# The last steps of a two-layer attention kernel: the last pair's projections first, four output products behind them, one pair's residuals in the place of the normalised x

## The chip, the core and the metric

The kernel runs on one core of a Trainium2 chip. A core has five engines that run side by side, each taking its instructions in the order in which they stand: PE multiplies matrices and writes to PSUM (eight banks), DVE does elementwise work and reductions, ACT applies functions such as exp and tanh, POOL does elementwise work on SBUF, and SP here issues the transfers. They wait for each other on semaphores. The metric is the time of one execution in microseconds (us); less is better.

## The reference

Two layers are applied to `x` of 32 sequences x 128 tokens x 512 features, both with a conditioning vector per sequence. The first is softmax attention with 16 heads, the second linear attention with 8 heads. The change touches the second alone:

```python
xn = _ln(x, ln_w, ln_b)
q = softmax((xn @ Wq + bq) per head, over the head's features)
k = softmax((xn @ Wk + bk + (1 - mask) * -1e6) per head, over the tokens)
v = (xn @ Wv + bv) * mask
att = einsum('bnhd,bnhl->bhdl', k, v)
y = einsum('bnhd,bhdl->bnhl', q, att)
scale, shift = split(silu(emb) @ W_emb + b_emb)
hh = _ln(y, ln2_w, ln2_b) * (1 + scale) + shift
return x + silu(hh) @ W_out + b_out
```

(The lines are those of the reference, with reshapes written out in words.) Everything is float32. Each large product is made of three faster ones, of high and low parts of both factors.

## The kernel before

The sequences are worked on in pairs (`GROUP = 2`), 16 pairs for each layer. The work of a pair is spread over three steps: in step `i` the pair `n = i + 2` is loaded, normalised and transposed, the pair `f = i + 1` is projected to keys, values and queries, and the pair `k = i` goes through attention, the second norm and the nonlinearity; the output products of the pair before come one step later still. The order on each engine is written out by hand, in one function per engine and step (`step0`, `step_mixed`, `step1`), and the steps of a layer run in a loop. Behind the last loop stands `drain(k, f)`: no pair is left to load, `k` is the last pair but one and `f` the last, and the output products of the pair `k - 2` are still due. The change is in these five `drain` functions (SP, POOL, ACT, DVE, PE).

The parts of it, as the rest of the text names them, with lines of the kernel before:

- PE: `keys`, `values`, `queries1` (24 products of 256 columns, or 12 of 512 for one sequence, L1294 to L1296), `turn_k` and `turn_q` (transposes, L1400 and L1408), `keys_values` (L1420: k times v, eight products), `query` (L1430: q times that), `turn_yn` (L1381), `output` (12 products of 512 columns, L1294 to L1296, with `s_hi` and `s_lo`).
- DVE: `k_soft` (L1001, L1006), `q_add` and `q_soft` (L1019 to L1028), `q_sums` (L1035, L1039), `kv_out` (L1048, scales the result of `keys_values`), `y_norm` (L960, then statistics at L894 and L898), `silu` (L976), `s_low_part` (L982), `output` (L988: adds product and residual).
- ACT: `k_exps`, `q_exps`, `kt_out`, `qt_out` (copies out of PSUM), `film1` (L657), `tanh` (L665), `s_high` (L670).
- POOL: `norm2` (L468 to L495), `v_mask` (L501, L505), `residual` (L521: adds the output bias to the residual).
- SP: `load_back` (L338, the residual into `x_res`), `store` (L342).

`LATE`, `LATER` and `DRAIN` name the PSUM banks that these steps use. `xn` is the buffer of the normalised x. `x_res` has room for one pair of residuals; `x_in`, where x was loaded for the norm, still holds the last pair's x and serves as its residual. Before, a residual of the pair `k` can therefore be loaded only when the finished output of the pair `k - 2` has been stored from the same place (`load_back` waits for `stored`). Buffers of one place that decide the order: `y_s` (the input of the second norm) and `th` (tanh and silu) hold one sequence each, so that `y_norm` of a sequence waits for `norm2` of the one before, and `silu` for the `s_high` and `s_low_part` of the one before.

## Time and profile before

| | us |
|---|---|
| median of 3 runs | 1080.86 (1080.82 to 1081.48) |
| the profiled execution, its own time | 1084.61 |
| its span, first to last instruction | 1082.8 |
| PE busy | 1030.0 (95%) |
| DVE busy | 770.1 (71%) |
| ACT busy | 609.6 (56%) |
| POOL busy | 588.7 (54%) |
| mean granted TensorE clock | 0.991 |

The span is the time from the first to the last instruction of the profiled execution. An engine counts as busy while it executes; matmuls overlap, so the time that one takes in a row is longer than the distance to the next one's start, and the distance is what a sequence of them costs. The drain runs from 1026.97 us to the end.

### The profile page before, as it was taken

Reading aid. Unit: us, or ns where it says so; the run is one execution under the profiler, and the core shown is the slowest. Engines: PE = TensorE matmul, PEld = TensorE weight load, DVE = VectorE, ACT = ScalarE, POOL = GpSimd, SP = SyncE. Lnnn points to the kernel's source line nnn. Section 1 sums busy time; section 2 is a strip of 40 time slices with the busy share of each in tenths; the row PEclk is TensorE's granted clock in tenths of the full one; section 3 lists DMA queues with packets and bytes.
Section 4 is the critical chain, followed back from the end, with each engine's and each line's share of the span. In section 5 each row is a group of like instructions: output and inputs, shape, how many; then the busy total and the mean of one; then the engine's idle time right before and its main releaser. Section 6 shows DMA issues by size and latency. Waiting matters only on the chain. (4 is left out here: it accounts for less than half of the span.)

```text
span 1082.8 us, 26060 instructions
## 1 busy us (share of the span) xinstructions
PE 1030.0 (95%) x8554; PEld 897.0 (83%) x8554; DVE 770.1 (71%) x1349; ACT 609.6 (56%) x2018; POOL 588.7 (54%) x870
## 2 busy tenths in 40 slices
PE   2999999999999999999997899999999999999996
PEld 2678889888888888988886778888888888888885
DVE  3567666766667666676678687777887787778775
ACT  2375678766776668766694544444444444444443
POOL 3453465445654465544653576556655565666623
PEclk9999999999999999999999899999999999999999
DMA  7833102211012110111113312222111121112111
GB/s 210 283 138 120 62 26 63 63 41 61 24 63 63 41 55 30 63 54 50 43 45 112 103 44 65 64 65 63 54 39 62 53 63 53 53 63 63 44 40 39
DMA packets 46401, 74.24 MB, mean 69 GB/s; under 512 B 8304, under 2 KB 14576, under 8 KB 46352
## 3 DMA queue, kind: packets, MB, share of 16 engines
q1 hardware_dynamic: 46352, 73.63, 21.4%
q8 instruction: 26, 0.43, 0.2%
q14 instruction: 23, 0.19, 0.1%
HBM read 56.80 MB, written 16.81 MB: 68 GB/s over the span
## 5 line engine op out<-in xcount | busy, mean ns | idle before, releaser
L468 POOL TENSOR_SCALAR stat<-stat 128x1 f32<-128x1 f32 x128 | 34.9, 273 | 351.5 <-DVE stat L898 330.4
L1294 PE MATMUL bank<-xt_hi,w_hi 128*128 128x256 f32 x768 | 220.4, 287 | 1.5 <-DVE xt_lo L921 1.5
L1296 PE MATMUL bank<-xt_hi,w_lo 128*128 128x256 f32 x768 | 215.5, 281 | 0.0
L1295 PE MATMUL bank<-xt_lo,w_hi 128*128 128x256 f32 x768 | 215.4, 281 | 0.0
L634 ACT ACTIVATE prob<-prob,neg_max 128x128 f32<-128x128 f32 x512 | 198.5, 395 | 10.5 <-DVE neg_max L935 10.5
L1294 PE MATMUL bank<-w_hi,xt_hi 128*128 128x512 f32 x384 | 157.2, 409 | 3.6 <-DVE w_lo L859 2.0
L1296 PE MATMUL bank<-w_hi,xt_lo 128*128 128x512 f32 x384 | 151.9, 396 | 0.0
L1295 PE MATMUL bank<-w_lo,xt_hi 128*128 128x512 f32 x384 | 151.3, 394 | 0.0
L1294 PEld LDWEIGHTS bank<-xt_hi,w_hi 128*128 128x128 f32 x768 | 146.5, 191 | 5.0 <-issue 1.9
L1295 PEld LDWEIGHTS bank<-xt_lo,w_hi 128*128 128x128 f32 x768 | 146.1, 190 | 1.3
L1296 PEld LDWEIGHTS bank<-xt_hi,w_lo 128*128 128x128 f32 x768 | 145.9, 190 | 0.0
L1294 PE MATMUL bank<-w_hi,s_hi 128*128 128x512 f32 x256 | 107.1, 418 | 4.1 <-DVE s_lo L982 2.7
L665 ACT ACTIVATE th<-z_s 128x512 f32<-128x512 f32 x64 | 40.9, 638 | 115.8 <-POOL z_s L511 115.2
L657 ACT ACTIVATE z_s<-bank,film_ab 128x128 f32<-128x128 f32 x128 | 48.1, 455 | 97.2 <-PE bank L1381 94.0
L521 POOL TENSOR_TENSOR x_res<-x_res,wide 128x512 f32<-128x512 f32 x62 | 91.5, 1486 | 18.3 <-DMA x_res<-between_layers 18.3
L1296 PE MATMUL bank<-w_hi,s_lo 128*128 128x512 f32 x256 | 101.2, 396 | 0.0
L1295 PE MATMUL bank<-w_lo,s_hi 128*128 128x512 f32 x256 | 100.7, 393 | 0.0
L634 ACT ACTIVATION_READ_ACCUMULATOR prob<-prob,neg_max 128x1 f32 x512 | 99.2, 194 | 0.0
L677 ACT ACTIVATE q_t<-q_t,k_max 128x128 f32<-128x128 f32 x128 | 49.9, 391 | 86.5 <-DVE k_max L1006 86.4
L932 DVE TENSOR_TENSOR prob<-bank,mask_row 128x512 f32<-128x512 f32 x128 | 87.6, 684 | 11.5 <-PE bank L1340 10.7
L935 DVE TENSOR_REDUCE neg_max<-prob 128x4 f32<-128x512 f32 x128 | 87.8, 686 | 4.4
L642 ACT ACTIVATE room<-bank 128x512 f32<-128x512 f32 x128 | 74.2, 593 | 29.3 <-PE bank L1351 28.3
(113 smaller groups left out, 2341.8 us busy)
## 6 DMA issues: line engine op xcount, KB each, us to landing
x_in<-in_x_dram SPq DMA_DIRECT2D x32, 256.0 KB, 2.8
x_res<-in_x_dram SPq DMA_DIRECT2D x32, 256.0 KB, 2.9
between_layers<-x_res SPq DMA_DIRECT2D x32, 256.0 KB, 2.0
x_in<-between_layers SPq DMA_DIRECT2D x32, 256.0 KB, 3.2
x_res<-between_layers SPq DMA_DIRECT2D x30, 256.0 KB, 2.6
out_dram<-x_res SPq DMA_DIRECT2D x30, 256.0 KB, 2.0
room<-in_L_cond_W_emb_dram SPq DMA_DIRECT2D x8, 512.0 KB, 6.9
prob<-in_L_cond_emb_w_dram SPq DMA_DIRECT2D x4, 512.0 KB, 7.6
```

Of the source, the lines that this page charges most:

```text
L468: pool.tensor_scalar(v[:, 8:9], v[:, 7:8], EPS, None, ALU.add).then_inc(s[a_in].sem, 1)
L521: pool.tensor_tensor(buf[:, b, :], buf[:, b, :], wide[:, OUT_BIAS[l], :], ALU.add).then_inc(s["res_full"].sem, 1)
L634: last = act.activation(prob[:, b, i, :], prob[:, b, i, :], ACT.Exp, bias=neg_max[:, b, i:i + 1], accum_out=row_sum[:, b, h:h + 1])
L642: act.activation(prob_t[:, g, :], bank[FIRST["PT"][g % 2]][:], ACT.Copy).then_inc(s[f"pt_out{g}"].sem, 1)
L657: last = act.activation(z_s[:, b, c * P:(c + 1) * P], bank[bk["H"][b]][:, c * P:(c + 1) * P], ACT.Identity, bias=shift, scale=scale)
L665: act.activation(th[:], z_s[:, b, :], ACT.Tanh, scale=0.5).then_inc(s["tanh_full"].sem, 1)
L677: last = act.activation(v[:, i, :], v[:, i, :], ACT.Exp, bias=k_max[:, pair, i:i + 1], accum_out=k_sum[:, slot, pair, i:i + 1])
L932: dve.tensor_tensor(prob[:, b, heads, :], bank[c][:].rearrange("p (r n) -> p r n", r=HC0), row, ALU.add).then_inc(s[f"masked{c}"].sem, 1)
L935: dve.tensor_reduce(neg_max[:, b, heads], prob[:, b, heads, :], AX.X, ALU.max, negate=True).then_inc(s[f"neg{c}"].sem, 1)
L1294: pe.matmul(o, a_hi, b_hi, start=start, stop=False)
L1295: pe.matmul(o, a_hi, b_lo, start=False, stop=False)
L1296: return pe.matmul(o, a_lo, b_hi, start=False, stop=stop)
```

## The change

It moves instructions in the drain and gives two residuals another place:

- PE: `keys(f, 0)` stands at the head, the two output products of the pair `k - 2` move behind `turn_q(f, 0)` and `query(f, 1)`, `turn_yn(k, 0)` and `(k, 1)` behind the `keys_values` of the pair `f`, and each `turn_yn` of `f` one product forward, so that the last four products are `LATER` 0 and 1 and `DRAIN` 0 and 1. The banks are given out anew.
- DVE, ACT: the same parts in a new order that follows PE. On DVE `k_soft(f, 0)` stands ahead of `kv_out(k, 0)`, and the `y_norm` of `f` behind `silu(k, 0)` and `s_low_part(k, 0)`.
- SP: the residuals of the pair `k` are loaded into `xn`, both at once, as soon as `xn` has been transposed; they no longer wait for the stores of the pair `k - 2`.
- POOL: both residual additions of `k` stand behind `norm2(k, 1)`. A wait of POOL on its own `consts` before the start is taken out.

Three places in the order of instructions. On PE, the end of the last loop step and the start of the drain (`q_t` and `room` are keys and queries being transposed), before:

```order
L1400 MATMUL bank<-ident,q_t 128x128 x4
L1408 MATMUL bank<-ident,room 128x128 x4
L1400 MATMUL bank<-ident,q_t 128x128 x4
L1294 MATMUL bank<-w_hi,s_hi 128x512
L1295 MATMUL bank<-w_lo,s_hi 128x512
```

and with the change (line numbers of the new kernel are one higher here):

```order
L1401 MATMUL bank<-ident,q_t 128x128 x4
L1409 MATMUL bank<-ident,room 128x128 x4
L1401 MATMUL bank<-ident,q_t 128x128 x4
L1295 MATMUL bank<-xt_hi,w_hi 128x256
L1296 MATMUL bank<-xt_lo,w_hi 128x256
```

The output product (`w_hi,s_hi`) that stood behind the third transpose is gone from there, and the key projection (`xt_hi,w_hi`) follows it directly.

On DVE, from the last `kv_out` to the first `silu` of the last pair (`prob` and `room` hold the matrices of k, v and q, `th` is tanh and silu), before:

```order
L1048 TENSOR_TENSOR prob<-bank,k_rec 64x4x64 x4
L960 TENSOR_TENSOR y_s<-bank,q_rec 128x512
L894 BN_STATS stat<-y_s 128x6
L898 BN_AGGR stat<-stat 128x2
L976 SCALAR_TENSOR_TENSOR th<-th,z_s 128x512
L982 TENSOR_TENSOR s_lo<-th,s_hi 128x512
L1035 TENSOR_REDUCE q_sum<-room 128x8
L1039 RECIPROCAL q_rec<-q_sum 128x8
L960 TENSOR_TENSOR y_s<-bank,q_rec 128x512
L894 BN_STATS stat<-y_s 128x6
L898 BN_AGGR stat<-stat 128x2
L988 TENSOR_TENSOR x_res<-bank,x_res 128x512
```

and with the change:

```order
L1036 TENSOR_REDUCE q_sum<-room 128x8
L1040 RECIPROCAL q_rec<-q_sum 128x8
L989 TENSOR_TENSOR x_res<-bank,x_res 128x512
L977 SCALAR_TENSOR_TENSOR th<-th,z_s 128x512
L983 TENSOR_TENSOR s_lo<-th,s_hi 128x512
L961 TENSOR_TENSOR y_s<-bank,q_rec 128x512
L895 BN_STATS stat<-y_s 128x6
L899 BN_AGGR stat<-stat 128x2
L961 TENSOR_TENSOR y_s<-bank,q_rec 128x512
L895 BN_STATS stat<-y_s 128x6
L899 BN_AGGR stat<-stat 128x2
L977 SCALAR_TENSOR_TENSOR th<-th,z_s 128x512
```

Both `y_norm` (`y_s` and its statistics) of the last pair now stand one behind the other, behind the first `silu` and `s_lo`; the second `q_sum` stands ahead of them.

On POOL, around the last `v_mask` (`mask_now`, `v_s`), before:

```order
L495 TENSOR_SCALAR yn<-y_s,stat 128x512
L521 TENSOR_TENSOR x_res<-x_res,wide 128x512
L501 COPY mask_now<-mask_col 128x1
L505 TENSOR_SCALAR v_s<-v_s,mask_now 128x512
L521 TENSOR_TENSOR x_in<-x_in,wide 128x512 x2
```

and with the change:

```order
L497 TENSOR_SCALAR yn<-y_s,stat 128x512
L523 TENSOR_TENSOR xn<-xn,wide 128x512 x2
L503 COPY mask_now<-mask_col 128x1
L507 TENSOR_SCALAR v_s<-v_s,mask_now 128x512
L523 TENSOR_TENSOR x_in<-x_in,wide 128x512 x2
```

The two additions of the pair `k` now stand side by side in `xn` ahead of the mask, where one in `x_res` stood; the other had stood at the head of the drain.

The diff:

```diff
--- before.py
+++ after.py
@@ -168,9 +168,9 @@
 
         MIXED = FIRST | dict(K=(6, 7), V=(0, 1), Q=(3, 4))
 
-        LATE = dict(O=(5, 3))
-        LATER = dict(O=(6, 3))
-        DRAIN = SECOND | dict(V=(0, 6), Q=(2, 2), KT=(4, 5), QT=(1, 0), KV=(4, 5), Y=(2, 1), H=(0, 4), O=(5, 7))
+        LATE = dict(O=(1, 2))
+        LATER = SECOND | dict(H=(5, 7), O=(5, 6))
+        DRAIN = SECOND | dict(V=(0, 3), Q=(2, 4), KT=(6, 7), QT=(2, 4), KV=(0, 3), Y=(6, 0), H=(3, 4), O=(7, 0))
 
         LAST_OUT = dict(O=(None, 1))
 
@@ -431,10 +431,12 @@
                 load_mask_pair(n)
 
             def drain(k, f):
+
                 for b in range(GROUP):
-                    store(1, k + (b - GROUP), b)
-                    load_back(1, k, b)
-                for at, buf in ((k, x_out), (f, x_in)):
+                    sp.wait_ge(*done(s["xn_turned"], f + b))
+                    sp.wait_ge(*done(s["res_full"], k + (b - GROUP)))
+                    sp.dma_start(xn[:, b, :], sequence(middle, k + (b - B))).then_inc(s["res_in"][b].sem, 16)
+                for at, buf in ((k + (-GROUP), x_out), (k, xn), (f, x_in)):
                     for b in range(GROUP):
                         store(1, at + b, b, buf)
 
@@ -512,7 +514,7 @@
                                    ).then_inc(s["z_full"].sem, 1)
 
             def residual(l, k, b, buf=x_res):
-                if buf is x_res:
+                if buf is not x_in:
                     pool.wait_ge(*landed(s["res_in"], k, b))
                 else:
 
@@ -568,18 +570,17 @@
                 v_mask(f, slot, 1)
 
             def drain(k, f):
-                residual(1, k, 0)
                 norm2(k, 0)
                 v_mask(f, 1, 0)
                 norm2(k, 1)
-                residual(1, k, 1)
+                residual(1, k, 0, xn)
+                residual(1, k, 1, xn)
                 v_mask(f, 1, 1)
                 residual(1, f, 0, x_in)
                 residual(1, f, 1, x_in)
                 norm2(f, 0)
                 norm2(f, 1)
 
-            pool.wait_ge(consts, 1)
             start()
             steps(pool, step0, (0,))
             loop(pool, step0, *LOOPS[0])
@@ -816,16 +817,16 @@
                 k_exps(f, 1, 0)
                 k_exps(f, 1, 1)
                 q_exps(f, 1, 0)
-                film1(k, 0)
-                tanh(k, 0)
                 kt_out(f, 0, DRAIN)
                 kt_out(f, 1, DRAIN)
+                q_exps(f, 1, 1)
+                qt_out(f, 0, DRAIN)
+                film1(k, 0, LATER)
+                tanh(k, 0)
+                qt_out(f, 1, DRAIN)
                 s_high(k, 0)
-                film1(k, 1)
-                qt_out(f, 0, DRAIN)
+                film1(k, 1, LATER)
                 tanh(k, 1)
-                q_exps(f, 1, 1)
-                qt_out(f, 1, DRAIN)
                 s_high(k, 1)
                 for b in range(GROUP):
                     film1(f, b, DRAIN)
@@ -1195,11 +1196,10 @@
                 s_low_part(k, 1)
 
             def drain(k, f):
-                output(LATE, k + (-GROUP), 0)
                 q_sums(k, 0, 0)
                 q_sums(k, 0, 1)
+                k_soft(f, 1, 0)
                 kv_out(k, 0, 0)
-                k_soft(f, 1, 0)
                 k_soft(f, 1, 1)
                 y_norm(1, k, 0, 0)
                 kv_out(k, 0, 1)
@@ -1208,25 +1208,26 @@
                 k_inverse(f, 1)
                 q_add(DRAIN, f, 0)
                 q_soft(f, 1, 0)
-                output(LATE, k + (-GROUP), 1)
+                v_add(1, DRAIN, f, 1, 1)
                 q_sums(f, 1, 0)
-                v_add(1, DRAIN, f, 1, 1)
-                silu(k, 0)
-                s_low_part(k, 0)
                 q_add(DRAIN, f, 1)
                 q_soft(f, 1, 1)
                 kv_out(f, 1, 0, DRAIN)
                 kv_out(f, 1, 1, DRAIN)
+                q_sums(f, 1, 1)
+                output(LATE, k + (-GROUP), 0)
+                silu(k, 0)
+                s_low_part(k, 0)
                 y_norm(1, f, 1, 0, DRAIN)
+                y_norm(1, f, 1, 1, DRAIN)
                 silu(k, 1)
+                output(LATE, k + (-GROUP), 1)
                 s_low_part(k, 1)
-                q_sums(f, 1, 1)
-                y_norm(1, f, 1, 1, DRAIN)
-                output(LATER, k, 0)
                 silu(f, 0)
+                output(LATER, k, 0, xn)
                 s_low_part(f, 0)
-                output(LATER, k, 1)
                 silu(f, 1)
+                output(LATER, k, 1, xn)
                 s_low_part(f, 1)
                 output(DRAIN, f, 0, x_in)
                 output(DRAIN, f, 1, x_in)
@@ -1554,7 +1555,6 @@
                 turn_k(k, 0, 0)
                 turn_q(k, 0, 0)
                 turn_k(k, 0, 1)
-                output(1, LATE, k + (-GROUP), 0)
                 keys(1, f, 1, 0)
                 turn_q(k, 0, 1)
                 keys_values(k, 0, 0)
@@ -1564,23 +1564,24 @@
                 values(1, DRAIN, f, 1, 0)
                 query(k, 1)
                 queries1(DRAIN, f, 1, 0)
-                output(1, LATE, k + (-GROUP), 1)
                 values(1, DRAIN, f, 1, 1)
-                turn_yn(1, k, 0)
                 turn_k(f, 1, 0, DRAIN)
                 turn_k(f, 1, 1, DRAIN)
                 queries1(DRAIN, f, 1, 1)
-                turn_yn(1, k, 1)
-                turn_q(f, 1, 0, DRAIN)
                 keys_values(f, 1, 0, DRAIN)
                 keys_values(f, 1, 1, DRAIN)
+                turn_yn(1, k, 0, LATER)
+                turn_q(f, 1, 0, DRAIN)
+                output(1, LATE, k + (-GROUP), 0)
+                turn_q(f, 1, 1, DRAIN)
                 query(f, 0, DRAIN)
-                turn_q(f, 1, 1, DRAIN)
+                turn_yn(1, k, 1, LATER)
                 query(f, 1, DRAIN)
+                output(1, LATE, k + (-GROUP), 1)
+                turn_yn(1, f, 0, DRAIN)
                 output(1, LATER, k, 0)
-                turn_yn(1, f, 0, DRAIN)
+                turn_yn(1, f, 1, DRAIN)
                 output(1, LATER, k, 1)
-                turn_yn(1, f, 1, DRAIN)
                 output(1, DRAIN, f, 0)
                 output(1, DRAIN, f, 1)
```

## Rows read from the trace of the kernel before

**Rows 1.** Stretches: time, busy per engine (instructions), PE clock, DMA share, GB/s.

```profile
1026.97:1079.60 52.63, 47.56 (x314) 39.91 (x312) 35.07 (x62) 23.12 (x58) 15.35 (x25) 0.97 0.10 36
1060.11:1063.52 3.41, 2.90 (x12) 2.53 (x12) 2.04 (x5) 0.27 (x2) 0.46 (x1) 0.50 0.00 0
```

**Rows 2.** PE in order of time: start us, us, engine, line, operation, count [idle before].

```profile
1028.20 0.48 PE L1294 MATMUL bank<-w_hi,s_hi 128*128 128x512 f32 x1
...
1031.05 0.28 PE L1294 MATMUL bank<-xt_hi,w_hi 128*128 128x256 f32 x1
...
1037.87 1.06 PE L1430 MATMUL bank<-prob 128*128 128x128 f32 x8
1038.85 0.69 PE L1420 MATMUL bank<-v_s,prob 128*64 128x64 f32 x16
1039.47 0.51 PE L1294 MATMUL bank<-w_hi,xt_hi 128*128 128x512 f32 x1
...
1048.75 0.39 PE L1294 MATMUL bank<-w_hi,xt_hi 128*128 128x512 f32 x1
...
1051.94 1.04 PE L1400 MATMUL bank<-ident,q_t 128*128 128x128 f32 x8
1052.73 0.48 PE L1294 MATMUL bank<-w_hi,xt_hi 128*128 128x512 f32 x1
...
1055.57 0.60 PE L1381 MATMUL bank<-ident,yn 128*128 128x128 f32 x4
...
1060.32 2.05 PE L1430 MATMUL bank<-prob 128*128 128x128 f32 x8 [1.82 <-issue]
...
1076.59 0.47 PE L1294 MATMUL bank<-w_hi,s_hi 128*128 128x512 f32 x1 [0.45 <-DVE s_lo L982]
```

**Rows 3.** DVE in order of time, the same columns.

```profile
1028.47 1.29 DVE L921 TENSOR_TENSOR xt_lo<-bank,xt_hi 128x512 fp32r<-128x512 f32 x2 [1.78 <-ACT xt_hi L605]
...
1032.98 0.68 DVE L988 TENSOR_TENSOR x_res<-bank,x_res 128x512 f32<-128x512 f32 x1
1033.59 0.68 DVE L1035 TENSOR_REDUCE q_sum<-room 128x8 f32<-128x512 f32 x1
...
1035.44 0.85 DVE L1048 TENSOR_TENSOR prob<-bank,k_rec 64x256 f32<-64x256 f32 x2
...
1038.07 0.88 DVE L1001 SCALAR_TENSOR_TENSOR q_t<-bank,col,mask_pair 128x256 f32<-128x256 f32 x2
...
1039.64 0.68 DVE L960 TENSOR_TENSOR y_s<-bank,q_rec 128x512 f32<-128x512 f32 x1
...
1043.78 0.69 DVE L960 TENSOR_TENSOR y_s<-bank,q_rec 128x512 f32<-128x512 f32 x1 [0.53 <-POOL yn L495]
...
1048.95 0.69 DVE L988 TENSOR_TENSOR x_res<-bank,x_res 128x512 f32<-128x512 f32 x1 [0.61 <-PE bank L1296]
...
1062.40 0.69 DVE L960 TENSOR_TENSOR y_s<-bank,q_rec 128x512 f32<-128x512 f32 x1 [1.29 <-PE bank L1430]
...
1064.09 0.69 DVE L976 SCALAR_TENSOR_TENSOR th<-th,z_s 128x512 f32<-128x512 f32 x1
```

**Rows 4.** POOL in order of time, around the last mask.

```profile
1056.13 0.64 POOL L501 COPY mask_now<-mask_col 128x1 f32<-128x1 f32 x1
...
1057.63 2.94 POOL L521 TENSOR_TENSOR x_in<-x_in,wide 128x512 f32<-128x512 f32 x2
```

**Rows 5.** DVE in order of time, in the chain of the last sequence.

```profile
1074.36 0.69 DVE L976 SCALAR_TENSOR_TENSOR th<-th,z_s 128x512 f32<-128x512 f32 x1 [0.77 <-ACT th L665]
1075.76 0.69 DVE L982 TENSOR_TENSOR s_lo<-th,s_hi 128x512 fp32r<-128x512 f32 x1 [0.70 <-ACT s_hi L670]
```

**Rows 6.** ACT in order of time, in the same chain.

```profile
1071.64 0.63 ACT L670 ACTIVATE s_hi<-th 128x512 fp32r<-128x512 f32 x1 [1.11 <-DVE th L976]
1072.18 1.49 ACT L657 ACTIVATE z_s<-bank,film_ab 128x128 f32<-128x128 f32 x4
...
1075.09 0.63 ACT L670 ACTIVATE s_hi<-th 128x512 fp32r<-128x512 f32 x1 [0.76 <-DVE th L976]
```

## The prediction

> **What bounds the kernel now.** I read three views: the stretch table for the whole drain and for one piece of it, then the instructions of PE in order of time through the drain, then those of DVE, ACT and POOL beside them. The stretch table [rows 1] says that PE is busy 47.56 of the 52.63 us of the drain, so about 5 us of PE's time is not work; it also says that from 1060.11 to 1063.52 the granted clock was 0.50. PE in order of time [rows 2] shows where the pauses are: from 1031.05 to 1055.57 the large matmuls stand one behind the other without a gap, then PE waits 1.82 us before `query(f, 0)` at 1060.32, which takes 2.05 us for eight passes where the same work at 1037.87 took 1.06. So the last pair's `query` comes late, and it comes late because DVE makes `kv_out(f)` only after a long queue. Behind it stands a chain in which PE hardly matters: y_norm on DVE, norm2 on POOL, a transpose, film1 and tanh on ACT, silu on DVE, s_high on ACT, s_low on DVE. It ends at 1076.59 with the last output product [rows 2], and 6.2 us after that the span is over; the change leaves this last piece as it is. What counts is therefore at what time the last output product starts: 1076.59 before.
>
> **Step 1, the start of the drain: a pause appears.** Before, `output(LATE, k-2, 0)` stood at the head, from 1028.20 to 1031.05 [rows 2]. Behind it `keys(f, 0)` found its input ready: xt_low was finished at 1028.47 + 1.29 = 1029.76 [rows 3]. Now `keys(f, 0)` stands at the head itself, and waits for xt_low(f, 1). A result of DVE reaches PE 0.14 us after it ends (s_low 1075.76, plus the 0.69 of its row, is 1076.45; the product starts at 1076.59 [rows 2, 5]). So `keys(f, 0)` starts at 1029.90: **a new pause of 1.7 us**, and still 1.15 us earlier than the old 1031.05.
>
> **Step 2, the stretch up to `queries1(f, 1)`.** From `keys(f, 0)` to `query(k, 0)` PE takes 1037.87 - 1031.05 = 6.82 us, so it arrives at 1036.72. `query(k, 0)` needs kv_out(k, 0) of DVE. There the output at 1032.98 is gone, which brings everything behind it forward by 1033.59 - 1032.98 = 0.61 [rows 3]; but k_soft(f, 0) now stands ahead of kv_out(k, 0). It starts at 1035.44 - 0.61 = 1034.83, takes 1039.64 - 1038.07 = 1.57, kv_out takes 0.85: 1037.25, and PE sees it at 1037.39. **A second new pause of 0.67 us.** The rest of the stretch is the same work: before, 1031.05 to 1055.57 is 24.52 us without a gap; of it `output(LATE, 1)` (one block of twelve 512-wide products, 1055.57 - 1052.73 = 2.84) and `turn_yn(k, 0)` (half of the eight transposes, 0.79 / 2 = 0.40) now stand behind. 24.52 - 3.24 = 21.28. So `queries1(f, 1)` ends at 1029.90 + 21.28 + 0.67 = **1051.85**, where it ended at 1055.57.
>
> **Step 3, what the last pair waits for then.** `keys_values(f, 0)` and `(f, 1)`, each 1039.47 - 1038.85 = 0.62, follow at 1051.85 and 1052.47. The second needs v_mask(f, 1) of POOL, ahead of which two residual additions now stand. y_norm(k, 0) starts at 1037.25 + 1.57 = 1038.82, and from one y_norm to the next, norm2 between them, is 1043.78 - 1039.64 = 4.14 [rows 3]: y_norm(k, 1) at 1042.96, its norm2 done at 1046.90; the pair of additions 2.94, the mask pair 1057.63 - 1056.13 = 1.50 [rows 4]: 1051.34. Margin over a microsecond, so I cost the move at nothing; the cover is gone if the additions take a microsecond more. The residuals of the pair k lie in `xn`, whose last reader is done by 1028.2; they are wanted only after 1046.90, and nothing is late if their load takes several times what it took. Before, the second residual load stood behind a store, and its addition and then v_mask(f, 1) were late by that: this wait goes.
> The kv_out(f) pair is now free of the 1.82 us wait: its DVE queue holds q_add and q_soft alone, which overlap PE's `turn_yn(k, 0)`, `turn_q(f, 0)` (0.79 together) and `output(LATE, 0)` (2.84). PE ends that product at 1051.85 + 1.24 + 0.79 + 2.84 = 1056.72. The fall of the clock that came behind the old wait should go too.
>
> **Step 4, the chain to the end.** DVE must finish output(LATE, 0) before silu(k, 0), and s_low(k, 0) before y_norm(f, 0). The end of a block reaches DVE after 0.20 (1048.75 to 1048.95 [rows 2, 3]): 1056.92. Then output 0.61: silu(k, 0) at 1057.53; from silu to s_low 1075.76 - 74.36 = 1.40 [rows 5]; s_low 0.61; so y_norm(f, 0) at **1059.54**, against 1062.40 before. That is 2.86 us of lead. From there: 4.14 to y_norm(f, 1), 1063.68; 1064.09 - 1062.40 = 1.69 to silu(k, 1), 1065.37; 0.73 to s_high (1074.36 to 1075.09), 0.54 to film1(f, 0) (1071.64 to 1072.18), 1066.64; 2.91 to its s_high (1072.18 to 1075.09), 1069.55 [rows 5, 6]; and 1076.59 - 1071.64 = 4.95 to the last product: **1074.50**. The chain before had silu(k, 1) and s_high ahead of y_norm(f, 1), overlapping norm2; now y_norm(f, 1) waits for norm2(f, 0) first and silu(k, 1) comes behind it, which gives back 0.8 of the lead. PE has, between y_norm(f, 0) and the end, pauses that this chain makes and that cost nothing: it finishes `output(LATE, 1)` at about 1062.2 and `turn_yn(f, 0)` can run only at 1063.6. After that three products of 2.84 would bring it to the last at 1073.1, so the chain, not PE, sets the end. What bounds the gain from above: with no chain at all PE could start the last product at 1062.2 + 0.8 + 3 x 2.84 = 1071.5, 5.1 us earlier than before.
>
> **The sum.** 1074.50 - 1076.59 = **-2.09 us**. On the profiled execution's span 1082.8 gives 1080.7, and its own time 1084.61 (1.8 more than the span) would be 1082.5. The median of the runs without a profile is 1080.86, 3.75 below the profiled one; I take the difference over unchanged: **1078.8 us**. Each handover is good to 0.05 and there are some fifteen, so the case itself reaches from 1077.8 to 1079.5. The removed wait on `consts` costs nothing either way: POOL waits next for the statistics of the first x, which a load precedes.
>
> **Rivals.** (1) *The clock falls in the new pause.* The stretch at 0.50, that is 1.2 GHz in place of 2.4 [rows 1], came after PE had stood still for 1.82 us and shortly before that for some tenths [rows 2]; the new pause of 1.7 us is nearly as long, and PE runs only transposes right ahead of it. Against it: it is one pause, not two, and large products follow. Price: 3.4 us at half the clock lose 1.7 us of dense work, of which the 0.67 pause before `query(k, 0)` takes up its own size: +1.0, so -1.1 in all, 1079.8; with both the pause and the low stretch badly placed 1080.5. The row at 1060.32 shows a fall behind a single long gap. The Trainium skill says in "TensorE: Matmul & The Clock Gate", What's actually happening, that the throttled state is the default and that activity releases it; by that rule a pause with only small work ahead of it is the place where the clock falls, and this rival's time would come out rather than the forecast's.
> (2) *Nothing is won.* The move of the additions ahead of v_mask(f, 1), or a late qt_out(f, 0) on ACT, holds up `query(f, 0)` or silu(k, 0) by the 2.1 us that were won. The margin of a microsecond on POOL speaks against it. 1080.9.
> (3) *Slower: half clock that holds.* PE goes to half clock in the pause at 1028, and again in the one that the chain makes at 1062 (some 1.4 us), and stays there for two such stretches each time. The first costs 2 x 1.7 - 0.67 = 2.7. The second falls on the products behind `turn_yn(f, 0)`, which have 1.4 us of slack up to 1074.50: 3.4 - 1.4 = 2.0. Together -2.1 + 2.7 + 2.0 = +2.6, so 1083.5. It decides from about 6.5 us at half clock in all; the one fall in the drain before lasted 3.4 us and ended by itself under this kind of work, which speaks against it.
>
> **How the numbers follow.** The forecast 0.62, rival 1 0.25, rival 2 0.08, rival 3 0.05. A difference under 0.2%, 2.16 us, is about what a measurement of this kernel can't tell from none, and the forecast of -2.1 lies right at that bound: of its 0.62 I give 0.31 to each side, and lean a little to the faster one, since the old execution's clock fall may weigh more without a profile than in it. Faster by over 0.2% 0.36, within 0.2% 0.59, slower 0.05. The range takes in the forecast's own width and rival 1 with its bound of 1080.5: 1077.7 to 1080.6.
>
> **What would show it.** On PE a pause up to about 1029.9 before the first 256-wide product, one of 0.7 before `query(k, 0)`, no pause before `query(f, 0)`, one of 1.4 before `turn_yn(f, 0)`; y_norm(f, 0) on DVE at about 1059.5; the last product at 1074.5; granted clock 1.00 throughout. I am wrong if the clock row shows 0.50 after 1029, if v_mask(f, 1) ends after 1052.3, or if the last product starts after something other than s_low(f, 1).

## The result, and the profile after the change

The changed kernel takes **1079.03 us** (median of 15 runs, 1077.29 to 1080.60), where the kernel before took 1080.50 beside it (15 runs, 1078.97 to 1083.82). The ratio is 0.9984 with an interval of [0.9977, 0.9991]: 1.7 us faster by the ratio (1.5 by the two medians), at least 1.0 and at most 2.5. That is inside the range and 0.2 us from the forecast time. The interval excludes that nothing changed, but the gain stays below the 0.2% that the prediction set as its bound.

The profiled execution is the one of 1078.31 us, with a span of 1076.3 and a granted clock of 0.997; before it was 1084.61 and a span of 1082.8. The spans differ by 6.5 us, three times what was forecast, so the first thing to read is where they differ. The stretch table splits each into the part ahead of the drain, where the two kernels run the same code but for POOL's first wait, and the drain. Of the kernel before (time, then busy us and instructions of PE, PEld, DVE, ACT and POOL, PE clock, DMA share, GB/s):

```profile
0.00:1026.97 1026.97, 982.40 (x8242) 857.04 (x8243) 734.30 (x1286) 586.46 (x1961) 573.34 (x846) 0.99 0.22 70
1026.97:1082.80 55.83, 47.56 (x314) 39.91 (x312) 35.77 (x63) 23.12 (x58) 15.35 (x25) 0.97 0.11 38
```

and of the kernel after:

```profile
0.00:1022.50 1022.50, 977.36 (x8242) 853.68 (x8243) 734.35 (x1286) 585.88 (x1961) 573.31 (x846) 1.00 0.22 71
1022.50:1076.30 53.80, 46.09 (x314) 38.52 (x312) 35.36 (x63) 22.96 (x58) 14.64 (x25) 1.00 0.11 40
```

The drain went from 55.83 to 53.80 us, **-2.03**, where -2.09 had been forecast. The other 4.47 lie ahead of it: the same 8242 matmuls took 982.40 us there in one execution and 977.36 in the other. That is not put down to the change: two kernels whose code ahead of the drain is that of before began it at 1020.11 and 1023.35, and one with that of after at 1027.03 (the last section comes back to it). POOL's first wait was not tested by itself; a difference from it would be lost in that scatter. So from here on kernels are compared by their drain, from the transposes at its start ([rows 1] begin there) to the end of the span, and beside that by their timed ratio.

Times of after are 4.47 lower than those of before for the same place in the drain. PE in order of time, the rows that answer to [rows 2] (start us, us, engine, line, operation, count [idle before it <- who released it]):

```profile
1025.43 0.36 PE L1295 MATMUL bank<-xt_hi,w_hi 128*128 128x256 f32 x1 [1.46 <-DVE xt_lo L922]
...
1032.90 1.13 PE L1431 MATMUL bank<-prob 128*128 128x128 f32 x8 [0.42 <-issue]
...
1047.59 1.15 PE L1421 MATMUL bank<-v_s,prob 128*64 128x64 f32 x32
...
1052.79 1.06 PE L1431 MATMUL bank<-prob 128*128 128x128 f32 x8
...
1059.23 0.63 PE L1382 MATMUL bank<-ident,yn 128*128 128x128 f32 x4 [1.29 <-POOL yn L497]
...
1063.85 0.63 PE L1382 MATMUL bank<-ident,yn 128*128 128x128 f32 x4 [1.22 <-POOL yn L497]
...
1070.10 0.47 PE L1295 MATMUL bank<-w_hi,s_hi 128*128 128x512 f32 x1
```

These are all of PE's pauses in the drain up to its last product, but for some tenths. The two new ones at its start are there, at `keys(f, 0)` and at `query(k, 0)`; `query(f, 0)`, at 1052.79, has none, and takes 1.06 us, not 2.05. Before both `turn_yn` of the last pair PE waits for POOL. The last output product starts at 1070.10, 0.15 behind the end of the last s_low below, as before.

DVE in order of time, what answers to [rows 3] and [rows 5]:

```profile
1052.56 0.69 DVE L989 TENSOR_TENSOR x_res<-bank,x_res 128x512 f32<-128x512 f32 x1
1053.16 0.68 DVE L977 SCALAR_TENSOR_TENSOR th<-th,z_s 128x512 f32<-128x512 f32 x1
1054.55 0.69 DVE L983 TENSOR_TENSOR s_lo<-th,s_hi 128x512 fp32r<-128x512 f32 x1 [0.70 <-ACT s_hi L671]
1055.16 0.68 DVE L961 TENSOR_TENSOR y_s<-bank,q_rec 128x512 f32<-128x512 f32 x1
...
1059.29 0.69 DVE L961 TENSOR_TENSOR y_s<-bank,q_rec 128x512 f32<-128x512 f32 x1 [2.41 <-POOL yn L497]
...
1060.98 0.69 DVE L977 SCALAR_TENSOR_TENSOR th<-th,z_s 128x512 f32<-128x512 f32 x1
...
1069.26 0.69 DVE L983 TENSOR_TENSOR s_lo<-th,s_hi 128x512 fp32r<-128x512 f32 x1
```

Here stands the chain of Step 4: output, silu, s_low, the first y_norm of the last pair, then 2.41 us in which DVE waits for norm2, the second y_norm, and only then silu(k, 1).

### The profile page after: what moved, and what is told of

It reads as the page before. It is cut to its first block and busy times, and to the rows that moved or that the text cites. A ratio compares the mean times of both kernels' runs of the same rounds, so it can differ in the third digit from the quotient of the medians.

```text
span 1076.3 us, 26062 instructions
## 1 busy us (share of the span) xinstructions
PE 1023.4 (95%) x8554; PEld 892.2 (83%) x8554; DVE 769.7 (72%) x1349; ACT 608.8 (57%) x2018; POOL 588.0 (55%) x870
## 5 line engine op out<-in xcount | busy, mean ns | idle before, releaser
L523 POOL TENSOR_TENSOR x_res<-x_res,wide 128x512 f32<-128x512 f32 x60 | 88.7, 1487 | 0.0
```

The costliest lines, as they stand in the source:

```text
L523: pool.tensor_tensor(buf[:, b, :], buf[:, b, :], wide[:, OUT_BIAS[l], :], ALU.add).then_inc(s["res_full"].sem, 1)
```

## The experiments

All run the same shapes and compute the same output; three of them do extra work that nothing reads, and say so. "Drain" is always the stretch defined above: 55.83 before, 53.80 after. Four kernels (dve_longer, pe_longer, late0_head, kv_first) ran once only, so that they have a drain and no ratio; and each drain but those of before and after is read from one execution.

### Does each kernel repeat? before_again and after_again

Both unchanged.

> The kernel before, unchanged, in a second profiled execution. What is asked: do its drain and the fall of the clock in it belong to the kernel, or to the one execution that was read? If they belong to the kernel: from the first transposes of the drain to the end of the span 55.8 us, within 0.15, with a pause of 1.8 us before the first query of the last pair and a stretch of some 3 us at half clock right behind it; where the drain starts (1019.8 to 1027.0 in the kernels so far) says nothing of it. If the fall belongs to the execution: no such stretch, and 54.9 to 55.0, what the filled pause gave; then 0.9 us of the 2.0 are chance and the change is worth 1.1. In the timed comparison with itself the ratio is 1.000 within 0.0010; a ratio further off would say how far a single comparison here can be trusted.

> The changed kernel once more, on the chip of the two others. If the drain is steady between executions and what lies ahead of it is not: the drain takes 53.8 within 0.1, while its start may lie anywhere between 1020 and 1027 as in the profiles so far.

The drain of before took 55.77 us in its second execution, that of after 53.84. The kernel before again paused and fell to half clock at the same place. PE and the stretch behind it:

```profile
1057.47 0.69 PE L1420 MATMUL bank<-v_s,prob 128*64 128x64 f32 x16 [0.59 <-POOL v_s L505]
1059.98 2.01 PE L1430 MATMUL bank<-prob 128*128 128x128 f32 x8 [1.83 <-issue]
```

```profile
1060.00:1063.30 3.30, 2.85 (x12) 2.45 (x12) 1.99 (x4) 0.41 (x1) 0.23 (x1) 0.50 0.00 0
```

So the drain repeats to within 0.1 us in both kernels, the fall of the clock in it too, and the difference of 2.0 is not chance. Two executions of each are all there is. The timed comparisons scatter more: before against itself gave 0.9998 [0.9987, 1.0010], after against before 0.9974 [0.9961, 0.9986] (medians 1077.82 and 1080.2) where the first comparison had given 0.9984. An edit worth a microsecond is read from the drain, not from the ratio.

### Which half of the change brings the gain? order_only and res_only

The change has two separable parts: the order of PE, DVE and ACT, and the place of the residuals of the pair `k`. order_only has the order of after, but loads the residuals into `x_res` behind the stores as before:

```diff
-                    sp.wait_ge(*done(s["xn_turned"], f + b))
-                    sp.wait_ge(*done(s["res_full"], k + (b - GROUP)))
-                    sp.dma_start(xn[:, b, :], sequence(middle, k + (b - B))).then_inc(s["res_in"][b].sem, 16)
-                for at, buf in ((k + (-GROUP), x_out), (k, xn), (f, x_in)):
+                    store(1, k + (b - GROUP), b)
+                    load_back(1, k, b)
+                for at, buf in ((k, x_out), (f, x_in)):
...
                 norm2(k, 1)
-                residual(1, k, 0, xn)
-                residual(1, k, 1, xn)
                 v_mask(f, 1, 1)
-                residual(1, f, 0, x_in)
-                residual(1, f, 1, x_in)
                 norm2(f, 0)
+                residual(1, k, 0)
                 norm2(f, 1)
+                residual(1, k, 1)
+                residual(1, f, 0, x_in)
+                residual(1, f, 1, x_in)
```

> The changed kernel with the residuals of the pair k back in x_res, each loaded behind the store of the pair k-2 and added on POOL behind norm2(f, 0) and norm2(f, 1), the x_in additions last (POOL's count of additions wants that order). Theory A: y_norm(f, 0) starts as early as in the changed kernel, but the additions now run on POOL beside the last silu and s_low on DVE, and the last residual is stored and loaded late: most of the 2.0 us is given back, 55.4 to 56. If the place of the residuals does not matter, 53.8.

Measured: drain 54.39, so -1.44 of the -2.03; ratio 0.9997 [0.9982, 1.0012]. PE's pauses are those of after, up to the last product:

```profile
1059.23 0.63 PE L1381 MATMUL bank<-ident,yn 128*128 128x128 f32 x4 [1.29 <-POOL yn L496]
...
1063.86 0.63 PE L1381 MATMUL bank<-ident,yn 128*128 128x128 f32 x4 [1.23 <-POOL yn L496]
...
1070.66 0.47 PE L1294 MATMUL bank<-w_hi,s_hi 128*128 128x512 f32 x1 [0.67 <-DVE s_lo L982]
```

Both `turn_yn` start within 0.01 us of where they start in after, and the last product at 1070.66 and not 1070.10: the place of the residuals costs 0.6 us, and only in the tail. It is not that the residuals come too late: DVE waits for none of them. What differs are two instructions of DVE, which run beside the additions that POOL now makes there. POOL makes them so late since it waits 3.25 us for the second load of `x_res`. DVE of order_only, and its POOL:

```profile
1067.88 0.92 DVE L976 SCALAR_TENSOR_TENSOR th<-th,z_s 128x512 f32<-128x512 f32 x1 [1.37 <-ACT th L665]
...
1069.50 1.01 DVE L982 TENSOR_TENSOR s_lo<-th,s_hi 128x512 fp32r<-128x512 f32 x1
```

```profile
1068.22 3.44 POOL L522 TENSOR_TENSOR x_in<-x_in,wide 128x512 f32<-128x512 f32 x2
```

silu(f, 1) takes 0.92 us, in after 0.69 (at 1067.87), and s_low(f, 1) 1.01, in after 0.69 (at 1069.26): together 0.55 of the 0.59. So my expectation had the place right (additions beside the last silu and s_low) and the price 1.0 to 1.6 us too high.

res_only is the other half: the order of before, the residuals of `k` in `xn`.

```diff
-                    store(1, k + (b - GROUP), b)
-                    load_back(1, k, b)
-                for at, buf in ((k, x_out), (f, x_in)):
+                    sp.wait_ge(*done(s["xn_turned"], f + b))
+                    sp.wait_ge(*done(s["res_full"], k + (b - GROUP)))
+                    sp.dma_start(xn[:, b, :], sequence(middle, k + (b - B))).then_inc(s["res_in"][b].sem, 16)
+                for at, buf in ((k + (-GROUP), x_out), (k, xn), (f, x_in)):
...
-                residual(1, k, 0)
                 norm2(k, 0)
                 v_mask(f, 1, 0)
                 norm2(k, 1)
-                residual(1, k, 1)
+                residual(1, k, 0, xn)
+                residual(1, k, 1, xn)
```

> The kernel before with one part of the change: the residuals of the pair k are loaded into xn and both are added on POOL behind norm2(k, 1); the order of PE, ACT and DVE stays. The drain, from its first transposes to the end of the span, took 55.83 us before and 53.82 with the whole change. Theory A (the chain that begins with the last pair's y_norm sets the end, and the order moved it forward): only the wait of 0.59 for v_mask(f, 1) goes, the pause of 1.8 before query(f, 0) stays, the drain takes 55.2. Theory B (what cost time was the residual load behind a store): the whole 2.0 us, 53.8. Theory C (the fall of PE's clock was the cost): as long as the pause stays, the clock falls again, 55.2 to 55.8.

Measured: drain **56.39**, longer than before by 0.56; ratio 1.0005 [0.9982, 1.0028]. The 0.59 us wait for v_s is gone, but PE then waits for DVE at the first query instead, and the clock is low for twice as long:

```profile
1052.83 1.47 PE L1431 MATMUL bank<-prob 128*128 128x128 f32 x8 [1.99 <-DVE prob L1049]
...
1055.92 2.05 PE L1431 MATMUL bank<-prob 128*128 128x128 f32 x8 [0.78 <-ACT prob L695]
```

```profile
1053.40:1060.30 6.90, 6.12 (x23) 5.20 (x23) 5.12 (x10) 1.23 (x2) 2.22 (x4) 0.51 0.00 0
```

None of the outcomes I had written down was this. The wait on the mask had been sitting in front of a wait on DVE, and taking it away merged the two pauses (0.59 + 1.82 became 1.99). The query did start sooner: 32.72 us after the start of the drain (1020.11 here), where it was 33.35 before; DVE's last subtraction ahead of `kv_out(f)` took 0.69 us and not 1.37, with no addition of POOL beside it. The first y_norm of the last pair is then 1.2 us earlier in the drain (34.22 for 35.43). The low stretch eats that and more, on PE: the first `turn_yn` of the last pair comes at 41.61, before at 40.76, with no pause in front of it in either kernel. DVE and PE of res_only, then PE of before:

```profile
1054.33 0.69 DVE L961 TENSOR_TENSOR y_s<-bank,q_rec 128x512 f32<-128x512 f32 x1 [0.72 <-PE bank L1431]
```

```profile
1061.72 0.60 PE L1382 MATMUL bank<-ident,yn 128*128 128x128 f32 x4
```

```profile
1067.73 0.60 PE L1381 MATMUL bank<-ident,yn 128*128 128x128 f32 x4
```

norm2 had ended at 1058.75 in res_only and at 1066.83 in before, so here it was PE, slowed by the low stretch, and not the chain that set the time. The two parts don't add: the place in `xn` is worth -0.6 with the new order and +0.6 without it.

### How much of the gain is the clock? fill_before

The kernel before, with eight products of 512 columns on PE in the pause ahead of `query(f, 0)`; they write a bank that the query overwrites, and nothing reads them.

```diff
-            def query(k, b, bk=SECOND):
+            def query(k, b, bk=SECOND, fill=0):
...
+                for j in range(fill):
+                    pe.matmul(bank[to][:], s_hi[:, 0, 0:P], hi[1][WO][:, j % C, :], start=True, stop=True)
...
-                query(f, 0, DRAIN)
+                query(f, 0, DRAIN, 8)
```

> The kernel before with eight more products of 512 columns on PE in the pause before query(f, 0), into the bank that query overwrites. They fill the 1.8 us and nothing else. Theory C: the granted clock stays at 1.00, query and the transposes behind it take 1.0 us instead of 2.05 for the pair, and the drain is 1.0 to 1.4 us shorter, 54.4 to 54.8. Theory A: the clock stays up too, but behind query the chain from y_norm(f, 0) sets the end; y_norm(f, 0) then starts 0.8 earlier, since query(f, 0) itself takes 0.9 instead of 1.8, so 55.0.

Measured: drain 54.95, -0.9 against before. The clock is 1.00 throughout and the query takes 1.05:

```profile
1056.67 1.05 PE L1432 MATMUL bank<-prob 128*128 128x128 f32 x8
...
1058.94 1.13 PE L1432 MATMUL bank<-prob 128*128 128x128 f32 x8 [0.78 <-ACT prob L694]
...
1066.99 0.63 PE L1381 MATMUL bank<-ident,yn 128*128 128x128 f32 x4 [0.96 <-POOL yn L495]
...
1072.08 0.47 PE L1294 MATMUL bank<-w_hi,s_hi 128*128 128x512 f32 x1 [1.34 <-DVE s_lo L982]
```

The pause is still there, filled; what went is the stretch at half clock. So, read from this one execution, 0.9 of the 2.0 us are the clock, and 1.1 is what is left for the earlier chain. A stretch of 3.4 us at half clock loses up to 1.7 us of PE's work, and the end moved by 0.9: the chain on DVE, ACT and POOL takes up the rest, as the last product shows, which now waits 1.34 us for s_low where it waited 0.45 [rows 2]. The timed ratio, 1.0007 [0.9994, 1.0019], doesn't show these 0.9 us: they would make 0.9992, which lies just outside the interval. Why is open, and with it how much of the timed gain of the change is the clock's.

### Chain or PE? dve_longer and pe_longer

The prediction says that after the change the chain behind y_norm(f, 0) sets the end and PE has slack. Both kernels are after with work added that nothing reads. dve_longer has two reductions (1.27 us together) on DVE ahead of y_norm(f, 0):

```diff
                 s_low_part(k, 0)
+                dve.wait_ge(*done(s["qsub"], f + 1))
+                for j in range(2):
+                    dve.tensor_reduce(neg_max[:, j, 0:H1], q_tmp[:].rearrange("p (h e) -> p h e", h=H1), AX.X, ALU.max)
                 y_norm(1, f, 1, 0, DRAIN)
```

> The changed kernel with two more reductions of 512 columns on DVE between s_low(k, 0) and y_norm(f, 0), whose results nobody reads; each takes DVE 0.6 to 0.7. Theory A (the chain that starts with y_norm(f, 0) sets the end): the whole 1.3 us shows, the drain takes 55.1 instead of 53.8. Rival (PE sets the end and the chain has slack): 53.8.

pe_longer has six products (1.4 us) at the front of `output(LATE, 1)`, ahead of the first `turn_yn` of the last pair:

```diff
-            def output(l, bk, at, b):
+            def output(l, bk, at, b, extra=0):
...
+                for kc in range(extra):
+                    three(bank[to][:], s_hi[:, b, kc * P:(kc + 1) * P], s_lo[:, b, kc * P:(kc + 1) * P],
+                          hi[l][WO][:, kc, :], lo[l][WO][:, kc, :], kc == 0, kc == extra - 1)
...
-                output(1, LATE, k + (-GROUP), 1)
+                output(1, LATE, k + (-GROUP), 1, 2)
```

> The changed kernel with six more products of 512 columns (1.37 us) on PE, ahead of output(LATE, 1) and into the same bank, which that product then overwrites. Theory A: they fill the pause of 1.29 before turn_yn(f, 0), the drain stays at 53.8 to 53.9. Rival (PE sets the end): 55.2.

dve_longer: drain 54.99, +1.19. pe_longer: drain 53.85, +0.05, for about the same amount of time on the other engine. PE of dve_longer, then of pe_longer, at the two `turn_yn`:

```profile
1060.13 0.63 PE L1385 MATMUL bank<-ident,yn 128*128 128x128 f32 x4 [2.48 <-POOL yn L497]
...
1064.94 0.60 PE L1385 MATMUL bank<-ident,yn 128*128 128x128 f32 x4
```

```profile
1058.67 0.63 PE L1382 MATMUL bank<-ident,yn 128*128 128x128 f32 x4
...
1063.29 0.63 PE L1382 MATMUL bank<-ident,yn 128*128 128x128 f32 x4 [1.23 <-POOL yn L497]
```

In pe_longer the pause of 1.29 has vanished into the added work and the end stands still; in dve_longer it has grown by the added work, and the end moved with it. That is shown, then: the chain sets the end, and PE has slack ahead of the first `turn_yn`. The pause of 2.48 us in dve_longer was followed by a stretch at half clock (0.52 from 1060.75 to 1064.15), but the 1.19 is not that: y_norm(f, 0) already starts 1.18 us later in the drain (33.84 for 32.66), ahead of the stretch, and silu(f, 0) 1.20. The row of y_norm(f, 0):

```profile
1056.05 0.68 DVE L961 TENSOR_TENSOR y_s<-bank,q_rec 128x512 f32<-128x512 f32 x1
```

### Is the first pause worth filling? late0_head

after with `output(LATE, 0)` back at the head of the drain, on PE and DVE: the pause before `keys(f, 0)` is filled, and 0.6 us of DVE are gone from the front of the chain.

```diff
-        LATE = dict(O=(1, 2))
+        LATE = dict(O=(5, 2))
...
             def drain(k, f):
+                output(LATE, k + (-GROUP), 0)
                 q_sums(k, 0, 0)
...
-                output(LATE, k + (-GROUP), 0)
                 silu(k, 0)
...
                 turn_k(k, 0, 1)
+                output(1, LATE, k + (-GROUP), 0)
                 keys(1, f, 1, 0)
...
-                output(1, LATE, k + (-GROUP), 0)
                 turn_q(f, 1, 1, DRAIN)
```

> The changed kernel with output(LATE, 0) back at the head of the drain on PE and DVE, where it stood before. The pause of 1.46 before keys(f, 0) is filled. Rival (that pause is lost time): 52.4. Theory A: that product then no longer covers q_soft(f, 1), the exponential and kv_out(f), two pauses of 1.1 come before turn_q(f, 1) and query(f, 1), y_norm(f, 0) is no earlier, 53.8 to 54.3.

Measured: drain 54.52, +0.7, outside what either side expected. PE:

```profile
1050.61 0.63 PE L1409 MATMUL bank<-ident,room 128*128 128x128 f32 x4 [0.88 <-ACT room L685]
...
1053.64 1.13 PE L1431 MATMUL bank<-prob 128*128 128x128 f32 x8 [0.98 <-ACT prob L695]
...
1059.24 0.63 PE L1382 MATMUL bank<-ident,yn 128*128 128x128 f32 x4 [1.71 <-POOL yn L497]
```

The pause at the start is gone and two others stand in the middle, before `turn_q(f, 1)` and `query(f, 1)`, both for ACT and both where they were expected. The output product had been the cover of ACT's exponentials and evictions there. On DVE silu(k, 0) now waits 0.64 us for tanh, and y_norm(f, 0) starts 0.61 later in the drain. So filling the pause at the start with this product costs 0.7 more than it brings; whether other work would fill it at a gain is not tested.

### Is more to be had from the chain? ynorm_only, kv_first, ynorm_kv

Step 4 says that y_norm(f, 1) ahead of silu(k, 1) gives back 0.8 us. ynorm_only puts the first y_norm of the last pair ahead of s_low(k, 0), and silu(k, 1) into the wait for norm2:

```diff
                 silu(k, 0)
-                s_low_part(k, 0)
                 y_norm(1, f, 1, 0, DRAIN)
-                y_norm(1, f, 1, 1, DRAIN)
+                s_low_part(k, 0)
                 silu(k, 1)
+                y_norm(1, f, 1, 1, DRAIN)
                 output(LATE, k + (-GROUP), 1)
```

> The changed kernel with one thing more on DVE: y_norm(f, 0) directly behind silu(k, 0), ahead of s_low(k, 0), and silu(k, 1) ahead of y_norm(f, 1). Theory A (the chain on DVE, POOL and ACT sets the end): y_norm(f, 0) starts 1.3 us earlier, silu(k, 1) and film1(f, 0) no longer wait for norm2(f, 0), the pause of 1.29 before turn_yn(f, 0) goes and the drain takes 51.8. Rival (PE or the stores set the end): 53.8 as with the change.

Measured: drain 53.16, only 0.64 less than after; ratio 0.9986 [0.9973, 0.9998]. The expectation of 51.8 was wrong by 1.4 us. PE of ynorm_only at the two `turn_yn`, and POOL at the second norm2, where the first norm2 of after takes 0.57 and 0.77:

```profile
1061.80 0.63 PE L1382 MATMUL bank<-ident,yn 128*128 128x128 f32 x4 [0.52 <-POOL yn L497]
...
1066.86 0.63 PE L1382 MATMUL bank<-ident,yn 128*128 128x128 f32 x4 [1.68 <-POOL yn L497]
```

```profile
1064.23 0.99 POOL L473 TENSOR_TENSOR stat<-stat,minus_half 128x1 f32<-128x1 f32 x1
1065.43 1.28 POOL L497 TENSOR_SCALAR yn<-y_s,stat 128x512 f32<-128x512 f32 x1 [0.21 <-POOL stat L473]
```

The first `turn_yn` came 0.77 sooner (its pause 0.52 for 1.29), and the second gave half of that back; the rest of the 0.64 is silu(k, 1), which is out of the way of the films, so that the last product no longer waits for s_low. From the second `turn_yn` on PE now works without a pause up to its end, so that only an earlier norm2 could still bring the end forward. Between the two y_norm now lie 4.64 us (1057.22 to 1061.86), not 4.13, and the second norm2 runs beside s_low and silu of DVE (1064.12 and 1065.55), where each of its two instructions takes 0.4 to 0.5 us longer. In after silu and s_low stand mostly beside other parts of this norm2, and the same two rows read:

```profile
1062.02 0.57 POOL L473 TENSOR_TENSOR stat<-stat,minus_half 128x1 f32<-128x1 f32 x1
1062.79 0.91 POOL L497 TENSOR_SCALAR yn<-y_s,stat 128x512 f32<-128x512 f32 x1 [0.21 <-POOL stat L473]
```

kv_first undoes one exchange of the change: kv_out(k, 0) goes ahead of k_soft(f, 0) on DVE again, against the second new pause.

```diff
                 q_sums(k, 0, 1)
-                k_soft(f, 1, 0)
                 kv_out(k, 0, 0)
+                k_soft(f, 1, 0)
                 k_soft(f, 1, 1)
```

> The changed kernel with kv_out(k, 0) back ahead of k_soft(f, 0) on DVE, as before the change. The pause of 0.42 before query(k, 0) goes, another of up to 0.5 comes before query(k, 1). The 0.3 us that PE is earlier reach the chain, since DVE's output(LATE, 0) waits for PE: 53.5. If the early pauses are made up for anyway: 53.8.

Measured: drain 53.47, -0.33; the pause before `query(k, 0)` is gone and all else stands 0.3 earlier. Its own time was 1083.22, since this execution's drain began at 1027.03: one profiled time of the whole kernel would have called it 4.9 us slower than after (1078.31).

ynorm_kv makes both edits.

> The kernel of ynorm_only with kv_out(k, 0) back ahead of k_soft(f, 0) on DVE. ynorm_only took 53.16 in the drain, kv_first 0.33 less than the changed kernel. If both gains reach the chain: 52.8, which is 3.0 under the kernel before, and a time some 0.28% under it. If the second is lost in the pauses of 0.52 and 1.68 before the two turn_yn of the last pair: 53.2.

Measured: drain 52.77, the sum of both gains to 0.1. Timed: 1076.77 us (11 runs), ratio to before **0.9972 [0.9962, 0.9982]**. It is the fastest of all, 3.0 us under the kernel before; beside after_again in the same comparison it is 1.05 us lower (1077.82), as the drains say (53.84 and 52.77).

### Is it the neighbour on DVE that slows norm2? slow_first

ynorm_kv with s_low(k, 1) ahead of y_norm(f, 1), so that it can't stand beside the second norm2:

```diff
                 silu(k, 1)
+                s_low_part(k, 1)
                 y_norm(1, f, 1, 1, DRAIN)
                 output(LATE, k + (-GROUP), 1)
-                s_low_part(k, 1)
                 silu(f, 0)
```

> The kernel of ynorm_kv with s_low(k, 1) ahead of y_norm(f, 1) and output(LATE, 1) behind it. In ynorm_only POOL's norm2(f, 1) took 2.96 instead of 2.05: its power took 0.99 and its last instruction 1.28 instead of 0.77, both beside s_low and silu of DVE. Theory D (DVE's instructions that read two SBUF tensors hold POOL up): with s_low out of the way the power takes 0.57, norm2(f, 1) 2.4 or less; y_norm(f, 1) starts 0.6 later, so the drain is the same as that of ynorm_kv within 0.3. Rival (the slowness has nothing to do with DVE): norm2(f, 1) stays at 2.9, and the drain is 0.6 longer.

Measured: drain 55.24, 2.5 longer than ynorm_kv, and no answer to the question. POOL, and PE behind it:

```profile
1060.61 0.99 POOL L473 TENSOR_TENSOR stat<-stat,minus_half 128x1 f32<-128x1 f32 x1
1061.81 1.32 POOL L497 TENSOR_SCALAR yn<-y_s,stat 128x512 f32<-128x512 f32 x1 [0.21 <-POOL stat L473]
```

```profile
1063.27 1.09 PE L1382 MATMUL bank<-ident,yn 128*128 128x128 f32 x4 [2.50 <-POOL yn L497]
```

norm2 is as slow as before the edit, since the silu of the last pair (1060.49) and its s_low (1061.87) moved into the place that was freed. For DVE idle beside the power there is the kernel before:

```profile
1069.52 0.57 POOL L471 TENSOR_TENSOR stat<-stat,minus_half 128x1 f32<-128x1 f32 x1
1070.30 0.78 POOL L495 TENSOR_SCALAR yn<-y_s,stat 128x512 f32<-128x512 f32 x1 [0.21 <-POOL stat L471]
```

DVE does nothing from 1069.49 to 1070.56 there, and the power takes 0.57 (in res_only as well); then silu starts beside the last instruction of norm2, and this time silu is the slow one, 1.05 us for 0.69. That speaks strongly for the neighbour as the cause. Which property of the neighbour does it, no run parts. What slow_first did show is the price of s_low on the path: y_norm(f, 1) came 0.8 us later in the drain than in ynorm_kv, PE paused for 2.50 us, and the clock fell to half for 3.4 us behind it.

## Why the prediction was right

**Step 1, the new pause.** `keys(f, 0)` was put at 1029.90, which is 1025.43 on the scale of after; it started at 1025.43. The row shows 1.46 us of idleness where I wrote 1.7, since I counted from the old start of the output product and the transposes ahead end 0.25 later. The time that counted, the start, was right.

**Step 2.** The second pause was forecast at 0.67 and is 0.42, by the same sort of counting: `query(k, 0)` should start at 1032.92 and did at 1032.90. `queries1(f, 1)` was to end at 1047.38; the products behind it start at 1047.59. Here 0.2 us were missing, in handovers between large products.

**Step 3.** Nothing waits for v_mask(f, 1), and kv_out(f) holds up nobody. The end of the mask was put at 1046.87; its row is 1045.76 + 0.69 = 1046.45. The fall of the clock went, as [rows 1] let one hope.

**Step 4, the chain.** On the scale of after, forecast and measured: silu(k, 0) 1053.06 and 1053.16; y_norm(f, 0) 1055.07 and 1055.16; y_norm(f, 1) 1059.21 and 1059.29; silu(k, 1) 1060.90 and 1060.98; last product 1070.03 and 1070.10. The offset of 0.1 comes in ahead of the chain and stays. dve_longer and pe_longer show that this chain and not PE sets the end. What bounded the kernel before was read too simply, though: "a chain in which PE hardly matters" is not what its rows show. norm2 of the first sequence of the last pair ended at 1066.83 and its transpose ran at 1067.73 without a pause ahead of it, since PE was still in an output product; res_only shows the same more strongly. The forecast didn't suffer, as it took only the end of that chain, 1076.59, from the trace. And the sentence of Step 4 that silu(k, 1) behind y_norm(f, 1) "gives back 0.8 of the lead" treated this as a plain debt: ynorm_only put silu back, with y_norm(f, 0) earlier besides, and won only 0.64, because norm2 on POOL is not of fixed length. The 4.14 from one y_norm to the next held in after (4.13) and not in ynorm_only (4.64).

**The sum.** -2.09 forecast, -2.03 in the drain, -1.7 [-2.5, -1.0] timed. What the prediction did not say is its composition: 0.9 of it is the fall of the clock that is no longer there (fill_before), which Step 3 named in half a sentence and Step 4 priced without naming it, since the old times it subtracts from already hold that fall. The other part, the earlier chain, is 1.1, by subtraction. It costed the move of the residuals at nothing and tested only POOL's margin; the move is worth 0.6 together with the new order, as without it POOL's additions fall beside the last silu and s_low, and it costs 0.6 alone.

**The last step** took the difference of one pair of executions over to the median. It held since the difference was summed within the drain, and with some luck: by the medians the gain is 1.5 us and not 2.1, but the kernel before came out 0.4 lower than in its first three runs, so that the time was hit within 0.2. By the ratio of after_again the gain is 2.8. The profiled spans themselves differ by 6.5 us, and whoever had compared these would have been off by a factor of three.

**The rivals.** (1) The clock didn't fall in the new pause, nor in its repetition after_again. The clock does fall in these drains behind longer pauses: it came behind 1.82, 1.83, 1.99, 2.48 and 2.50 us in the drains here, and not behind 1.46, 1.29, 1.22, 1.68 and 1.71. (2) Nothing held the gain up; POOL's margin was there. (3) No low stretch under work in the drain of after: the granted clock is 1.00 until 1075.7, and 0.50 only behind PE's last product. Two low stretches in a row, which this rival needed, do occur, in res_only (6.90 us).

## What to carry to other kernels

Price a reordering by following one chain of handovers from where the two orders part to the last product, each start from a row; that gave 0.1 us here, over fifteen steps. Then ask of each wait that is taken away what ends next behind it and what it does to the pauses: alone, the removed wait of 0.59 us merged with the one behind it, the clock was low for 6.9 us and not 3.4, and the drain got 0.56 longer although DVE was earlier. Work on an engine that is off the path can still be felt there: see POOL's additions in order_only. And compare traces by the stretch that differs, from a common event to the end, not by spans.

## What was not expected of the hardware

**The same pause may or may not drop the clock.** Halfway through the program both kernels have a pause of 1.98 us before the same product. In before's trace it is followed by a low stretch, in after's it isn't. PE of before and its stretch table, then PE of after:

```profile
608.58 0.50 PE L1294 MATMUL bank<-w_hi,xt_hi 128*128 128x512 f32 x1 [1.98 <-DVE w_lo L859]
```

```profile
609.60:613.00 3.40, 3.40 (x9) 2.67 (x8) 3.05 (x6) 3.40 (x17) 1.54 (x4) 0.51 0.00 0
```

```profile
605.37 0.50 PE L1295 MATMUL bank<-w_hi,xt_hi 128*128 128x512 f32 x1 [1.98 <-DVE w_lo L860]
```

In after_again the same product starts at 604.47 behind the same 1.98 us, and there the clock did fall (604.8 to 608.4). The length of the pause alone doesn't decide it, then. Ahead of the drain before's execution had five such stretches and after's two, and the drain began anywhere from 1019.83 (ynorm_kv, one stretch) to 1027.03 us (kv_first, four) in code that is the same but for POOL's first wait. The number of stretches goes with the start, but loosely: executions with two of them began their drains from 1020.11 to 1023.35. What else varies there stays open. The Trainium skill, "TensorE: Matmul & The Clock Gate", What's actually happening, says that activity releases the throttle; the low stretch above agrees, as it ended while PE was busy for all of its 3.40 us.

**POOL and DVE slow each other.** One-column arithmetic on POOL took 0.57 us beside an idle DVE and 0.99 in ynorm_only, a pass over 128x512 took 0.77 and 1.28, with s_low or silu of DVE (0.69 each) at the same time. The other way round, silu and s_low of DVE took 0.92 and 1.01 for 0.69 in order_only beside additions on POOL. norm2 stands in the chain twice, so it can cost there twice. The cause is read from what runs at the same time in kernels that differ in little else; slow_first, made to test it, failed to part it. Durations on POOL are rough in this profile, so its sizes are less sure than those on DVE.
